# First layer of a four-stage kernel: other step table, first rows made in the stage ahead, last batch by tiles, products in two halves

## What is computed

```python
x = x + _layernorm(_L0_attn_ref(_layernorm(x), Wq, Wkv, Wo))
x = x + _layernorm(_L0_ffn_ref(_layernorm(x), q_scales, q_vals, bias))
x = x + _layernorm(_L1_attn_ref(_layernorm(x), ...))
x = x + _layernorm(_L1_ffn_ref(_layernorm(x), ...))
```

```python
scores = einsum('bqhd,bkd->bhqk', q, k) * 0.25
scores = where(causal, scores + slopes[h] * (pos_k - pos_q), -inf)
out = einsum('bhqk,bkd->bqhd', softmax(scores), v).reshape(b, s, h) @ Wo
```

## Time and profile before

| what | us |
|---|---|
| median of 3 runs | 2539.72 |
| profiled execution | 2542.48 |
| its span, first to last instruction | 2540.7 |
| PE busy | 2095.1 (82%) |
| DVE busy | 1766.8 (70%) |
| ACT busy | 1381.7 (54%) |
| POOL busy | 1045.2 (41%) |
| the first layer, from 60.6 | to 844.3 |
| mean granted clock of PE | 0.92 |

### The profile page before, as it was taken

One profiled execution on the slowest core, in us unless ns is written; L12 is line 12 of the kernel. 1 busy time (PEld: TensorE's weight loads), 2 busy tenths in 40 slices (PEclk: granted clock), 3 DMA queues, 4 the chain that ended last, 5 costly groups with the idle time before them and its releaser, 6 DMA issues. The chain is left out here.

```text
span 2540.7 us, 46475 instructions
## 1 busy us (share of the span) xinstructions
PE 2095.1 (82%) x17280; PEld 1247.1 (49%) x17280; DVE 1766.8 (70%) x3729; ACT 1381.7 (54%) x3014; POOL 1045.2 (41%) x1043
## 2 busy tenths in 40 slices
PE   7477768667664479999999999999999999857997
PEld 3245545445442245555565655555556556423443
DVE  3489868778753367777777777777777777576554
ACT  2245544454543366667666776667666767341221
POOL 0058867678772243334333333334333334112221
PEclk9698889888877699999999999999999999979999
DMA  5101010100100333434434334443343333320000
GB/s 201 39 16 31 27 28 14 42 12 11 40 2 33 104 79 63 90 82 78 82 76 88 80 65 86 85 91 82 63 88 80 63 68 69 64 94 17 34 17 34
DMA packets 394621, 153.65 MB, mean 60 GB/s; under 512 B 362960, under 2 KB 373840, under 8 KB 392352
## 3 DMA queue, kind: packets, MB, share of 16 engines
q1 hardware_dynamic: 394400, 150.73, 26.1%
HBM read 48.69 MB, written 11.53 MB: 24 GB/s over the span
## 5 line engine op out<-in xcount | busy, mean ns | idle before, releaser
L1208 POOL TENSOR_TENSOR q_in_sbuf<-q_in_sbuf,sinq 128x512 f32<-128x512 f32 x128 | 231.5, 1809 | 688.9 <-ACT q_in_sbuf L1336 581.3
L1348 ACT ACTIVATE xp<-xp,nm 128x128 f32<-128x128 f32 (+3 forms) x512 | 281.3, 550 | 354.5 <-DVE nm L1427 354.5
L1398 DVE SCALAR_TENSOR_TENSOR probs_lo<-xp,rl,probs_hi 128x128 f16<-128x128 f32 (+3 forms) x512 | 263.2, 575 | 109.5 <-ACT probs_hi L1313 109.5
L714 ACT ACTIVATE weights<-bank,unit 128x512 f32<-128x512 f32 x320 | 210.7, 686 | 97.9 <-PE bank L556 91.6
L487 POOL CAST weights_hi<-weights 128x1024 f16<-128x1024 f32 (+1 forms) x192 | 205.6, 1091 | 124.8 <-ACT weights L714 124.5
L1427 DVE CUSTOM_DVE_ANT_0 xp<-bank,mask,cs 128x128 f32<-128x128 f32 (+3 forms) x512 | 250.1, 543 | 0.0
L1313 ACT ACTIVATE probs_hi<-xp,rl 128x128 f16<-128x128 f32 (+3 forms) x512 | 244.1, 549 | 0.7 <-DVE rl L1447 0.7
L1232 PE MATMUL bank<-xT_hi,wq_hi 128*128 128x512 f16 x512 | 196.7, 384 | 43.2 <-DVE yacc L1442 36.8
L1232 PE MATMUL bank<-p1T_hi,v_hi 128*128 128x128 f16 x1280 | 222.8, 220 | 3.0 <-DMA p1T_lo<-probs_lo 3.0
L1232 PE MATMUL bank<-p1T_lo,v_hi 128*128 128x128 f16 x1280 | 222.7, 220 | 0.0
L1232 PE MATMUL bank<-p1T_hi,v_lo 128*128 128x128 f16 x1280 | 222.7, 220 | 0.0
(11 more groups left out here) (286 smaller groups left out, 5763.2 us busy)
## 6 DMA issues: line engine op xcount, KB each, us to landing
raw_q<-in_wq SPq DMA_DIRECT2D x8, 1024.0 KB, 5.3
raw_o<-in_wo SPq DMA_DIRECT2D x8, 1024.0 KB, 5.5
x_front<-in_x SPq DMA_DIRECT2D x4, 1024.0 KB, 5.7
q_stack<-q_hi SPq DMA_DIRECT2D x256, 16.0 KB, 1.8
xb<-in_x SPq DMA_DIRECT2D x4, 1024.0 KB, 5.4
x_scratch<-xb SPq DMA_DIRECT2D x4, 1024.0 KB, 4.4
x_before<-x_scratch SPq DMA_DIRECT2D x4, 1024.0 KB, 5.6
wup<-in_wup SPq DMA_DIRECT2D x3, 1024.0 KB, 12.0
```

The costliest lines, as they stand in the source:

```text
L714: act.activation(px[:, p % 2, i, :], bank_of(("x", p, i))[:, :], ACT.Exp, scale=unit[:, 0:1]).then_inc(s_ed, 1)
L1208: pool.tensor_tensor(qs[:, i % 2, :], qs[:, i % 2, :], rope["sink" if u[0] == "k" else "sinq"][:, :], ALU.mult).then_inc(s_rot, 1)
L1348: ins = act.activation(x, x, ACT.Exp, scale=-1.0, bias=nm[:, m % 3, t:t + 1], accum_out=ls[:, m % 3, t:t + 1])
L1398: ins = dve.scalar_tensor_tensor(pr[1][:, m % 2, c], xp[:, m % 3, c], rl[:, m % 3, t:t + 1], pr[0][:, m % 2, c], ALU.mult, ALU.subtract)
```

## The change

- Stage ahead: the x rows of batch 0, `ident` and `rel` are loaded behind the first two fused loads; DVE makes the statistics before its maxima, POOL the iota, the slopes and rstd, ACT the norm and copies of fused tiles 0 to 3; PE transposes the rows between fused tiles 3 and 4; ACT and DVE make hi and lo of them, and DVE the constants, between its maxima and its splits (`middle`). Fused tiles 8 to 11 use the banks of the transposes.
- The table: steps from -6 to 78. Other steps for o, y, f, n2, n3, K and V. Variance in the step of `NORM`, rstd and ACT's norm one step later, adds of two rows at the end of the second and of two at the start of the third step.
- PE: K, q, y, f as first of the others are filled in two halves (2 slices of depth each) around score part 3; maxima are transposed at the end of the step, evacuated in the next, and stacked in SP's next step.
- In SP's list the queries of group g+2 now stand ahead of the maxima of group g.
- DVE takes both weights_lo of a pair one step after its exponentials; k_stack and k_stack_max are made by ACT; POOL's heads take two instructions a pair.
- The query stacks are started four at a time.
- The last batch behind its y runs by tiles, in banks 0 to 5 (`END`, `tail_variance`, `tail_add`), with DVE's add in place of POOL's, and four stores.

The diff, cut:

```diff
+            middle.get("vector", nothing)(dve)
...
-        STEPS = range(-20, NP + N_LAG + 26)
-        FRONT = {"load": -16, "norm": -11, "n1": (-8, -7), "V": -6, "K": -5}
-        BACK = {"load": 27, "o": (14, 17, 21, 26), "y": (28, 28, 29, 29), "add1": 30, "n2": (32, 34),
-                "f": (36, 36, 38, 38), "add2": 39, "n3": (46, 47)}
+        LAST = B - 1
+        STEPS = range(-6, NP + 15)
+        FRONT = {"load": -16, "n1": (-8, -7), "K": -6, "V": -5}
+        BACK = {"load": 27, "o": (14, 18, 22, 25), "y": (26, 27, 28, 28), "n2": (33, 34), "f": (35, 36, 37, 38),
+                "n3": (45, 46)}
+        NORM = {"n1": -13, "a1": 28, "n2": 31, "a2": 38, "n3": 41}
...
+        def has(kind, b):
+            return b > 0 if kind == "n1" else b < LAST if kind in ("f", "n2", "n3", "a1", "a2") else True
...
+            fillings["rest"] += others(n)
             if n % GP == 0 and 0 <= n // GP - 1 < NG:
                 fillings["rest"].append(("m", n // GP - 1))
-            fillings["rest"] += others(n)
-        groups = {"s": banks[0:3], "x": banks[3:6], "rest": banks[6:8]}
+        END = ([(k, LAST, t) for k, t in (("n2", 0), ("n2", 1), ("f", 0), ("n2", 2), ("f", 1), ("n2", 3), ("f", 2),
+                                          ("f", 3))] + [("n3", LAST, t) for t in range(TT)])
+        fillings["end"] = END
+        groups = {"s": banks[0:3], "x": banks[3:6], "rest": banks[6:8], "end": banks[0:6]}
...
-                    g, r = divmod(n, GP)
+                    g, r = divmod(n - 1, GP)
                     if r == 0 and 0 <= g - 1 < NG:
                         stack_maxima(g - 1)
                     g, r = divmod(n + 4, GP)
                     if r == 0 and 0 <= g < NG:
                         stack_queries(g)
-                    b = at(n, BACK["add2"] + 2)
-                    if b is not None:
+                    b = at(n, NORM["a2"] + 3)
+                    if b is not None and b < LAST:
                         sp.wait_ge(s_ad, TT * (add_no["a2", b] + 1))
                         sp.dma_start(x2_dram[b].rearrange("(t p) d -> p t d", p=P), xb[:, :, :]).then_inc(s_out, 16)
-                sp.wait_ge(s_out, 16 * B)
+                for t in range(TT):
+                    sp.wait_ge(s_ta, TT + t + 1)
+                    sp.dma_start(x2_dram[LAST, t * P:(t + 1) * P, :], xb[:, t, :]).then_inc(s_out, 16)
...
-                pool.iota(pos, [[1, S]], base=0, channel_multiplier=0, allow_small_or_imprecise_dtypes=True)
                 pool.memset(mx[:, :, :], 0.0)
                 pool.memset(v2[:, :, :, E0:EV], 1.0)
-                pool.memset(v2[:, :, :, EV + E0:2 * EV], 0.0)
-                for h in range(H0):
-                    ins = pool.memset(sl[:, h:h + 1], SLOPES[h])
-                ins.then_inc(s_io, 1)
+                pool.memset(v2[:, :, :, EV + E0:2 * EV], 0.0).then_inc(s_io, 1)
...
-                    for e in range(2):
-                        c, o = (2 * (p % PAIRS) + e) * E0, ob[:, p % 3, e, :, :]
-                        if p or e:
-                            pool.wait_ge(s_on, 2 * p + e)
-                        pool.tensor_tensor(od[:, :, :], o[:, :, 0:E0], o[:, :, EV:EV + E0], ALU.add).then_inc(s_os, 1)
-                        pool.wait_ge(s_os, 2 * p + e + 1)
-                        pool.tensor_tensor(on[:, :, c:c + E0], od[:, :, :],
-                                           ro[:, p % 3, e, :].unsqueeze(2).to_broadcast([P, TT, E0]),
-                                           ALU.mult).then_inc(s_on, 1)
+                    if p >= 1:
+                        pool.wait_ge(s_on, p)
+                    c, o = 2 * (p % PAIRS) * E0, ob[:, p % 3, :, :, :]
+                    pool.tensor_tensor(od[:, :, :, :], o[:, :, :, 0:E0], o[:, :, :, EV:EV + E0], ALU.add).then_inc(s_os, 1)
+                    pool.wait_ge(s_os, p + 1)
+                    pool.tensor_tensor(on[:, :, c:c + 2 * E0].rearrange("p t (e c) -> p e t c", e=2), od[:, :, :, :],
+                                       ro[:, p % 3, :, :].unsqueeze(3).to_broadcast([P, 2, TT, E0]),
+                                       ALU.mult).then_inc(s_on, 1)
...
-                pool.wait_ge(s_sc, 1)
                 for n in STEPS:
+                    for u in norms_at(n - 3):
+                        if u in add_no:
+                            add_rows(u, (2, 3))
+                    for u in norms_at(n - 1):
+                        rstd(norm_no[u])
+                    if 0 <= n - N_LAG < NP:
+                        norm_heads(n - N_LAG)
                     if 0 <= n - X_LAG < NP:
                         weights_hi(n - X_LAG)
-                    if 0 <= n - N_LAG < NP:
-                        norm_heads(n - N_LAG)
-                    for u in norms_at(n):
-                        rstd(norm_no[u])
+                    for u in norms_at(n - 2):
                         if u in add_no:
-                            add_rows(u)
+                            add_rows(u, (0, 1))
...
+                def half(u, i):
+                    kind, b = u[0], u[1]
+                    out = bank_of(u) if i else ready_bank(u)
...
-                pe.wait_ge(s_sc, 1)
                 for n in STEPS:
                     extra = others(n)
+                    if n == 0:
+                        pe.wait_ge(s_sc, 1)
                     turn(n, 0, 1)
                     if 0 <= n - V_LAG < NP:
                         weigh_values(n - V_LAG)
                     turn(n, 2)
-                    if n % GP == 0 and 0 <= n // GP - 1 < NG:
-                        turn_maxima(n // GP - 1)
+                    split = bool(extra) and extra[0][0] in ("K", "q", "y", "f")
                     for u in extra[:1]:
-                        fill(u)
+                        if split:
+                            half(u, 0)
+                        else:
+                            fill(u)
                     turn(n, 3)
+                    for u in extra[:1]:
+                        if split:
+                            half(u, 1)
                     for u in extra[1:]:
                         fill(u)
                     turn(n, 4)
+                    if n % GP == 0 and 0 <= n // GP - 1 < NG:
+                        turn_maxima(n // GP - 1)
+                pe.wait_ge(*emptied[fillings["s"][-1]])
+                pe.wait_ge(*emptied[fillings["x"][-1]])
+                for u in END:
+                    fill(u)
...
+                def stack_keys(b):
+                    for i, k in enumerate((kz, ks)):
+                        act.wait_ge(s_kb, 2 * b + i + 1)
+                        if b >= 2:
+                            act.wait_ge(*filled[("x", PAIRS * (b - 1) - 1, 4)])
+                        for e, half in enumerate(("even", "odd")):
+                            act.activation(k[:, b % 2, e, :], kb[:, i, :], ACT.Copy,
+                                           scale=row[half][:, 0:1]).then_inc(s_kr, 1)
...
+                        if i == 0 and (n - 1) % GP == 0 and 0 <= (n - 1) // GP - 1 < NG:
+                            maxima_hi((n - 1) // GP - 1)
+                        if i == 2 and 0 <= n - V_LAG < NP:
                             copy_heads(n - V_LAG)
-                        if i == 2:
-                            if n % GP == 0 and 0 <= n // GP - 1 < NG:
-                                maxima_hi(n // GP - 1)
+                        if i == 3:
                             for u in extra[:1]:
                                 evacuate(u)
-                        if i == 3:
+                        if i == 4:
                             for u in extra[1:]:
                                 evacuate(u)
-                    for u in norms_at(n):
+                    b = at(n, FRONT["K"] + 1)
+                    if b is not None:
+                        stack_keys(b)
+                    for u in norms_at(n - 1):
                         normalise(u)
+                    if -4 <= n < GP - 5:
+                        start_stack(n + 5)
...
+                        weights_lo(n - X_LAG - 1, 0)
+                    if (n - 1) % GP == 0 and 0 <= (n - 1) // GP - 1 < NG:
+                        maxima_lo((n - 1) // GP - 1)
...
+                    for u in norms_at(n):
+                        kind, b = u
+                        if kind == "n1":
+                            dve.wait_ge(s_xf, 16 * b)
                         for t in range(TT):
-                            statistics(t, xf)
-                        variance(("n1", b))
-                    for k, when in (("1", BACK["add1"]), ("2", BACK["add2"])):
-                        b = at(n, when)
-                        if b is not None:
-                            variance(("a" + k, b))
-                        b = at(n, when + 1)
-                        if b is not None:
-                            for t in range(TT):
-                                dve.wait_ge(s_ad, TT * add_no["a" + k, b] + t + 1)
+                            if kind == "n1":
```

(47 more changed lines are left out.)

385 lines of the change are left out of this document (254 added, 131 removed).

## The result

The changed kernel takes 2479.64 us in the median of 4 runs (2474.61 to 2483.16), where the kernel before takes 2541.89 beside it (2535.81 to 2546.15): a ratio of 0.9755, 95% interval 0.9726 to 0.9784. That is 62 us, of 118 forecast, and 1.6 us above the range. The profiled execution took 2481.93 us, its span is 2480.1, 60.6 less than before.

What follows compares the result with a forecast made beforehand. VectorE, busiest in the steady stretches, idles 118.7 us there; the ends are latency chains. -23.7+2-75-31 = -127.7, less 10 for TensorE's clock: -118, 2424.5 profiled, forecast 2422 us, range 2396 to 2478.

Steps and rivals of the forecast that it cites:

- start of the queries: Layer front: SyncE begins stacking queries at 74.9 instead of 98.58, -23.7 us, including +1.5 from the stage ahead.
- from there to step 8: First group: the +11.9 us stall, less a removed norm stall and shorter steps 6 and 7, leaves +2 by step 8.
- steps 8 to 64: Steady part: terms of -64-11-8-7-2+9 give -83 us, kept at -75 since stalls in one step overlap.
- end: Layer's end: heads_T_lo 19 us earlier and last-batch norms pipelined by tiles for 12; -31 us, bounds -15 and -40.
- put off for the clock: Whole sum: 10 us taken off the gain for steps whose bound passes to TensorE at 1.2 GHz.
- Step 6: First group: exponents wait for three query trains, a load and the maxima, about 51.1 us after the first query DMA; +11.9.
- maxima behind queries: SyncE's queue, later groups: about 3 us at three groups of the first batch, nothing later; +9, bounds 0 and +60.
- Rival A: SyncE's queue: maxima behind queries cost at every group, 4 us on average; +51, 2473 us, chance 0.14.
- Rival B: Steady part: POOL keeps the bound, norm stalls only half gone, halves and heads gain nothing; 2462 us, chance 0.12.
- norms: Steady part: rstd and ScalarE's norm a step later, so ScalarE does not wait; -64 us up to 709.7, lower bound -32.
- halves: Steady part: TensorE's products filled in halves around a score filling win half of 22 us; -11, bounds 0 and -20.
- heads: POOL's heads in two instructions a pair, 1.5 to 1.0 us; 0.25 us in some 30 light steps, -7, bounds 0 and -15.

Runs made afterwards that it cites:

- maxima first: Changed kernel with SyncE's stack_queries one step later, behind the maxima of the group ahead; 2458.54 us, ratio 0.9683.
- c1: On top of maxima first, a group's maxima are turned, evacuated and stacked in its first step, as in the kernel before; ratio 0.9592.
- c2: On top of maxima first, VectorE's first evacuation of a step moved behind its second weights_lo; ratio 0.9589.
- e1: Changed kernel with only VectorE's first evacuation of a step moved behind its second weights_lo; ratio 0.9697.
- four mends: Changed kernel with maxima ahead of queries, maxima's way as before, VectorE's first evacuation behind its second weights_lo, and two end edits; 2413.71 us, ratio 0.9505.
- c4: On top of maxima first, POOL scales heads ahead of rstd and VectorE takes the last batch's f products one slot earlier; ratio 0.9635.

## Why the prediction was wrong, point by point

The sign, the removed norm waits and the first stall were right; the steady part and the end were not. The span became 60.6 us shorter where 117.7 was the sum:

| part | forecast | measured | miss |
|---|---|---|---|
| start of the queries | -23.7 | -29.6 | -5.9 |
| from there to step 8 | +2 | +4.4 | +2.4 |
| steps 8 to 64 | -75 | -31.7 | +43.3 |
| end | -31 | -8.2 | +22.8 |
| put off for the clock | +10 | in the rows above | -10 |
| rest of the program | 0 | +4.5 | +4.5 |

**Front.** The layer starts 1.0 us earlier in place of 1.5 later; VectorE's last split ended at 53.8 (55.3 forecast), and the eight stores went out as one row of 5.03 us from 51.82. POOL's memset did not wait 9 us in the layer: its long wait, 8.15 us, lies in the stage ahead now, where it costs nothing. So the queries started at 69.0, not 74.9: 9.4 us behind the layer's start where 12.8 stood, a figure 0.5 to 1.5 above the forecast's own terms for it (6.1, 5.2 and up to 1). The Trainium skill ("GPSIMD Engine Reference", Instruction dispatch) has about 6 us for the first call to a freshly loaded kernel; the trace agrees in kind: the wait stands ahead of the first partition_all_reduce, which now comes behind an iota and elementwise work, with 7.4 of the 8.15 us behind VectorE's first maximum (17.42), and ahead of no memset.

**Step 6** was right: 51.7 us to ScalarE's first exponent, 50.9 to TensorE's, from which the forecast's 51.1 was counted. With maxima first, step 8 comes 4.7 us earlier after the first query DMA.

**The step that failed** is the sum of the steady part, -83 kept at -75, where 31.7 us came. It failed in two ways, and the larger one is terms that it put at nothing.

*Two waits that the change adds had no term.* The maxima's way, one step later, was treated as SyncE's matter alone. That m then holds one of two banks over the end of a step, and that exponents of light groups wait for m_lo even with the queue free, was not looked at: 23 us with the order mended (c1), 16.6 of them in the steady part. VectorE's evacuation stands in front of its second weights_lo, behind a product whose second half now comes later: 24 us with the order mended (c2), 17.5 in the steady part; 15 and 10.1 in the changed kernel (e1).

*The price of "maxima behind queries" for the groups after the first, +9, had the wrong working.* It was worked out as cover: an interval of 19.5 us against 17 us of steps as long as they were **before** the change, 7 us for a light one. The same change made light steps 6.0 us long and took the norm waits out of others, which was booked as a gain beside it. The same steps cannot be both. From q_lo to the start of step 18 there are 14.9 us (206.66 to 221.54), against the 19.7 that passed until its exponents, and the stall comes back in every round of the first batch, since it delays its own next q_lo. As a size the term was not far off: maxima first gives 13.3 us in the steady part and 18 in all, where 9, and 21 with step 6, had been put. What the forecast had missed is that this loop hides other things: while it holds, the maxima's way brings 3 us of its 23.

All four mends together bring 46.1 us of the steady part, where 43.3 were missed. Rival A (4 us in each of 15 groups, 2473, chance 0.14) had the order's cost with the right sign and its time came nearest, but that is luck: the order measured 18 us where A has about 72 with step 6, and the first batch paid nearly all of it. Rival B is out as a cause: ScalarE's waits for nb are gone.

**The terms themselves** came out near or above their size in the kernel with the mends: norms 72 for 64, halves 10 for 11, heads 17 for 7. In the changed kernel the norms show 45 to 48. The heads were mis-sized: the duration taken was the median of a lone instruction, but a pair's two cost 1.39 us in the mean in the kernel with the mends, and its four 2.0 (see below). The 8 for heads_T and the 2 for k_stack were not measured. Taken back one by one these three are worth 99 us by the ratios where 82 were put, so that the steady part of 472.5 falls near the forecast's 475 is in part two errors that cancel.

**End**: -8.2 for -31. heads_T_lo was to come 19 us earlier and came 2.1 earlier, counted from step 64. With POOL's adds behind the heads, the way from the last exponent to heads_T_lo did lose 9.7 us (23.6 to 13.9). But steps 64 to 70, first to last exponent, took 50.7 us where they were 43.1, for which the forecast had no term. Most of that is again the evacuation's place: with it behind the second weights_lo they take 44.3 (e1 and c2 alike), and the end 117.7 and 117.3. POOL's rstd ahead of the last heads is not what holds them, since in c4, with heads first, they came later. The way from the last y to the end was to lose 12 and lost 5.1; 4.5 more came with f ahead of the last transposes (c4).

**The 10 us** put off for TensorE's clock have no measurement of their own: no run separates TensorE's clock from the waits. The granted clock of steps 8 to 24 is 0.87 in the changed kernel and 0.93 with the mends, for the same products, so it is higher where the waits are gone.

Of the forecast's own signs: waits for nb under 15 us, yes (none listed); heads near 0.45, yes (0.418); step 6 standing still, yes; a middle batch of 135 to 145 us, no (152.8, and 148.9 even with the mends); last exponent to the layer's end under 75, just not (75.7, before 91.6); and long waits of TensorE for the maxima in later groups, named as the sign of being wrong, were there.

Still open: how much of the steps of 10 to 15 us in later batches, found in all kernels here, is TensorE's work at its lower clock; why c4 is 7.5 us shorter in the steady part; and which of the three waits that c1's edit removes made its 23 us.

## What to carry to other kernels

When a transfer is moved behind a train in the same queue, draw the loop from its data back to the train's next start and compare its length with the steps **as they will be**, not as they were; a cover that the same change shortens is no cover. Where two engines evacuate one bank in turn, the second one's place in its list matters as much as the product's, and a small product that is moved over the end of a step, with its bank and all that waits for it, is a cost to write down.
